# A segment sum in two levels: four 32-column matmuls and one that moves their result

## The chip, the cores and the metric

The kernel runs on one core of one Trainium2 chip. The metric is the device time of one execution in microseconds (us), of which the median over several runs is taken. Engines are named as in the profile: PE is TensorE's matmul, PEld its weight load, DVE is VectorE, ACT ScalarE, POOL GpSimd, SP SyncE.

## The reference

A graph layer (sum of the neighbours' features over 100,000 edges sorted by destination, 6,250 nodes of 256 features) and then a feed-forward layer with 8 experts, of which each node takes its best two.

```python
x = x + _L0_gnn_ref(_layernorm(x, axis=-1), W_self, W_neigh, b, src, dst)
x = x + _L0_ffn_ref(_layernorm(x, axis=-1)[None], gamma, beta, Wr, br, W1, b1, W2, b2)[0]

def _L0_gnn_ref(feat, W_self, W_neigh, b, src, dst):
    msg = feat[src]
    agg = jax.ops.segment_sum(msg, dst, num_segments=n)
    deg = jax.ops.segment_sum(jnp.ones_like(dst, dtype=feat.dtype), dst, num_segments=n)
    h_neigh = agg / jnp.maximum(deg, 1.0)[:, None]
    return feat @ W_self + h_neigh @ W_neigh + b

# feed-forward: the best 2 of 8 experts, weighted by a softmax over their two logits
logits = jnp.einsum('bsd,de->bse', xn, Wr) + br
h = jax.nn.gelu(jnp.einsum('bsd,dh->bsh', xn, W1[e]) + b1[e], approximate=False)
y_e = jnp.einsum('bsh,hd->bsd', h, W2[e]) + b2[e]
y = y + y_e * w_full[..., e, None]
```

All data are float32. The destinations are 6250 times the square of a uniform number, so edges lie dense at low nodes and thin at high ones.

## The kernel before

The edges stand in 784 columns of 128, sorted by destination. Four columns are a group (`GT = 4`), 196 groups in all, worked from the highest nodes down. POOL gathers a group's 512 source rows into a ring of four groups by four indirect DMAs (L689). DVE writes the group's one-hot matrices (L1257): for each edge a 1 in the column of its destination, counted from the group's first node (`target`), 128 columns wide. PE multiplies (L964): four accumulating matmuls give the sums of up to 128 nodes from the group's first on, and, from a column of ones, their degrees. DVE adds the result with two masks to the two blocks of 128 nodes that it may touch (`agg`, L1311), after which a block whose edges are all in is "finished": turned by PE (L952), multiplied with both weight matrices (L993, L995), normalised, routed (L1010), and its rows scattered to the experts' lists by POOL (L697).

Beside that run the experts. A unit is a tile of 128 listed rows with one expert, or a dense block with one expert. For each unit PE forms the hidden product (L1040, tiles and dense units alike), DVE adds the bias into `hid` (L1468), ACT applies gelu (L866), PE forms the result product (L1066 for tiles, L1074 for dense units), and DVE weighs it (L1477, L1479; L1499, L1503 for dense units). There is one hidden bank in PSUM, so a unit's hidden product waits for the bias of the unit before (`biased`). `hid` has two buffers.

What holds it together is a plan: `plan()` gives every step of every unit and block a slot, and each engine walks the slots in one loop, `for t in range(END)`, doing what falls into slot t in an order written out by hand. The 196 groups take slots 0 to 195. By these tables (`DENSE_STEPS`, `TILE_STEPS`) a unit's bias stands one slot after its hidden product; for the last 50 tiles both stand in the same slot. 143 of the 196 slots hold a hidden product, and 66 of these products stand in the slot in which DVE adds the bias of the unit before. A plan's slot has no fixed length; an engine passes on to the next as its waits allow.

The order inside a slot is: on PE turns, hidden product, places, router, block products, result product, and last the group sum; on DVE one-hots for group t+2, block steps, the bias, lists, choices, block sums, the weighing, and last the addition of group t-1 (`group_sums`). Groups 0 to 5 (`RAW`) are normalised by ACT after the gather. `claims()` at slot 3 counts edges that don't fit the assumptions about spans; were there any, a repair path would redo all edges.

## Time and profile before

| | us |
|---|---|
| median of 3 runs (1587.45, 1588.26, 1598.54) | 1588.26 |
| span of the profiled execution, first to last instruction | 1546.9 |
| PE busy | 1199.9 (78%) |
| DVE busy | 867.0 (56%) |
| ACT busy | 426.8 (28%) |
| POOL busy | 944.1 (61%) |
| mean granted TensorE clock | 0.908 |

The profiled execution's own time is not reported apart from these runs; its span is 41.4 us under their median. The busy time of an engine is a sum over its instructions in that one execution. A matmul's end is modelled and overlaps the next one's start. An fp32 matmul is listed as two records (x8 for four matmuls).

### The profile page before, as it was taken

The numbers are of one execution on the slowest core, as the hardware profiler recorded it, in microseconds if no ns is written. First come the engines' busy times: TensorE is split into PE (matmuls) and PEld (weight loads), VectorE is DVE, ScalarE is ACT, GpSimd is POOL, SyncE is SP. The second block draws the span as 40 slices with busy tenths as digits, with TensorE's granted clock in tenths as the row PEclk, the third lists the DMA queues.
The fourth block names the chain that finished last, engine by engine and source line by source line (L and its number), as shares of the span: only waits on it lengthen the run. The fifth ranks groups of instructions, "written<-read, shape, count | busy, mean of one in ns | idle before, by whom it ended". The sixth has DMA issues, their size and how long they took to land.

```text
span 1546.9 us, 22459 instructions
## 1 busy us (share of the span) xinstructions
PE 1199.9 (78%) x6492; PEld 1041.8 (67%) x6493; DVE 867.0 (56%) x2814; ACT 426.8 (28%) x803; POOL 944.1 (61%) x1023
## 2 busy tenths in 40 slices
PE   0377988888977798989889888677858775879857
PEld 0266777867866676877778777566747764778747
DVE  6745556665564655656565565554636553545426
ACT  5412222222322332332332323213313210211111
POOL 6756656666566666566655657665665566666642
PEclk9788999999997899999999999788978897999979
DMA  9798777755454565555554555464565556656545
GB/s 335 232 297 247 244 230 239 238 166 173 152 166 124 164 190 160 181 172 171 188 182 157 181 157 164 135 191 133 165 204 157 167 158 199 201 165 222 167 139 175
DMA packets 175355, 289.69 MB, mean 187 GB/s; under 512 B 25600, under 2 KB 105344, under 8 KB 175104
## 3 DMA queue, kind: packets, MB, share of 16 engines
q1 hardware_dynamic: 124288, 156.38, 30.6%
q0 software_dynamic: 45504, 124.36, 27.3%
q10 hardware_dynamic: 5440, 7.47, 1.4%
q8 instruction: 57, 0.93, 0.2%
q14 instruction: 66, 0.54, 0.1%
HBM read 231.43 MB, written 56.68 MB: 186 GB/s over the span
## 4 chain that ended last, share of the span: by engine, by line
PE 33%; DVE 28%; another core or an unknown queue 21%; issue 12%; DVEq 2%; POOL 2%; DMA 1%; SPq 0%; ACT 0%; POOLq 0%; ACTq 0%
PE bank L1040 9%; PE bank L964 8%; PE bank L1066 6%; DVE agg L1311 5%; PE bank L1074 4%; DVE heap L1468 4%; DVE onehot L1257 3%; PE bank L952 2%; PE bank L993 1%; PE bank L995 1%; DMA heap<-in_x 1%; DVE nstats L1339 1%; DVE xf L1334 1%; DVE agg L1337 1%
## 5 line engine op out<-in xcount | busy, mean ns | idle before, releaser
L689 POOL DMA_INDIRECT ring<-feature_table,src_sb x760 | 742.3, 977 | 468.3 <-issue 194.6
L964 PE MATMUL bank<-ring,onehot 128*128 128x257 f32 x1552 | 404.0, 403 | 73.5 <-DMA rows<-in_x,src_sb 40.9
L964 PEld LDWEIGHTS bank<-ring,onehot 128*128 128x128 f32 x1552 | 312.1, 203 | 131.7 <-issue 83.4
L1468 DVE TENSOR_TENSOR heap<-bank,b_sb 128x512 f32<-128x512 f32 x145 | 100.1, 690 | 342.1 <-remote 249.7
L1066 PE MATMUL bank<-heap 128*128 x712 | 193.5, 418 | 60.4 <-issue 18.1
L1040 PE MATMUL bank<-row_t,heap 128*128 128x128 f32 x1424 | 195.9, 294 | 38.8 <-DVE heap L1468 19.3
L1040 PEld LDWEIGHTS bank<-row_t,heap 128*128 128x128 f32 x1424 | 186.6, 208 | 46.2 <-issue 45.0
L866 ACT ACTIVATE heap<-heap 128x512 f32<-128x512 f32 x145 | 91.6, 632 | 453.7 <-DVE heap L1468 312.7
L1066 PEld LDWEIGHTS bank<-heap 128*128 128x128 f32 x712 | 142.4, 208 | 86.0 <-issue 66.3
L1040 PE MATMUL bank<-dst_i,heap 128*128 128x128 f32 x896 | 115.8, 284 | 32.8 <-DVE heap L1468 25.9
L1257 DVE TENSOR_TENSOR onehot<-iota,target 128x512 f32<-128x512 f32 x196 | 134.3, 685 | 6.9 <-DVE xf L1328 3.5
L1040 PEld LDWEIGHTS bank<-dst_i,heap 128*128 128x128 f32 x896 | 109.8, 198 | 41.4 <-issue 39.1
L1311 DVE SCALAR_TENSOR_TENSOR agg<-bank,in_first,agg 128x257 f32 x196 | 94.3, 481 | 75.1 <-remote 37.7
L1074 PE MATMUL bank<-heap 128*128 128x256 f32 x448 | 116.4, 404 | 21.3 <-DVE agg L1503 8.1
L859 ACT ACTIVATE row_t<-bank,gb_sb 128x128 f32<-128x128 f32 x178 | 71.8, 455 | 179.0 <-remote 106.6
L697 POOL DMA_INDIRECT expert_rows<-rows,slots_of x82 | 83.5, 1019 | 50.1 <-issue 23.0
L1074 PEld LDWEIGHTS bank<-heap 128*128 128x128 f32 x448 | 86.4, 201 | 35.8 <-issue 25.0
L1311 DVE SCALAR_TENSOR_TENSOR agg<-bank,in_second,agg 128x257 f32 x196 | 93.3, 476 | 0.0
L993 PE MATMUL bank<-wn_sb,sums_t 128*128 128x256 f32 x196 | 56.5, 411 | 18.8 <-issue 10.4
L844 ACT ACTIVATE normal_t<-bank,gb_sb 128x128 f32<-128x128 f32 x84 | 33.8, 452 | 130.7 <-remote 91.0
L826 ACT ACT_TABLE_LOAD x47 | 60.3, 1283 | 0.8
L866 ACT ACT_TABLE_LOAD x46 | 59.0, 1283 | 0.8
(190 smaller groups left out, 1258.1 us busy)
## 6 DMA issues: line engine op xcount, KB each, us to landing
heap<-in_w SPq DMA_DIRECT2D x145, 512.0 KB
expert_out<-empty_row SPq DMA_DIRECT2D x68, 256.0 KB
ring<-feature_table,src_sb POOLq DMA_INDIRECT x760
row<-expert_rows SPq DMA_DIRECT2D x89, 128.5 KB
xf<-in_x SPq DMA_DIRECT2D x49, 128.0 KB
ff<-feature_table SPq DMA_DIRECT2D x49, 128.0 KB
expert_out<-inside SPq DMA_DIRECT2D x45, 128.0 KB
expert_out<-y_out SPq DMA_DIRECT2D x44, 128.0 KB
```

The source lines that it names most:

```text
L689: pool.indirect_dma_start(group_row(t, i)[:, 0:D], None, x if t < RAW else table, bass.IndirectOffsetOnAxis(src_sb[:, k:k + 1], 0)).then_i ...
L697: pool.indirect_dma_start(rows_tab, bass.IndirectOffsetOnAxis(slots_at(S, n)[:, c:c + 1], 0), rows[s][:, c, :], None).then_inc(S.scattered ...
L859: last = act.activation(row_t[s][:, k, :], turned_b[:, k * P:(k + 1) * P], ACT.Identity, bias=gb_sb[:, 1, k:k + 1], scale=gb_sb[:, 0, k:k ...
L866: act.activation(hid[s], hid[s], ACT.Gelu).then_inc(S.gelu, 1)
L964: last = pe.matmul(bank[t % 2][:, 0:D + 1], onehot[:, q, i, :], group_row(t, i), start=(i == 0), stop=(i == GT - 1))
L993: pe.matmul(product_b[:, D:2 * D], t[:, k, :], wn_sb[:, k, :], start=(k == 0), stop=(k == DK - 1))
L1040: last = pe.matmul(hidden_b[:, c * P:(c + 1) * P], w1_of[w][:, k, c * P:(c + 1) * P], turned[:, k, :], start=(k == 0), stop=(k == DK - 1))
L1066: last = pe.matmul(result_b[:, 0:D], hid[s][:, k, :], w2_sb[:, k, bass.ds(e, 1), :].rearrange("p o d -> p (o d)"), start=(k == 0), stop=(k ...
L1074: last = pe.matmul(result_b[:, 0:D], hid[unit_of_dense[u] % 2][:, k, :], w2_sb[:, k, u % NE, :], start=(k == 0), stop=(k == HK - 1))
L1257: dve.tensor_tensor(onehot[:, q, :, :], iota[:, :].unsqueeze(1).broadcast_to([P, GT, P]), target[:, g * GT:(g + 1) * GT].unsqueeze(2).broa ...
L1311: last = dve.scalar_tensor_tensor(out=a, in0=bank[t % 2][:, 0:D + 1], scalar=mask[:, g:g + 1], in1=a, op0=ALU.mult, op1=ALU.add)
L1468: dve.tensor_tensor(hid[S.slot(u, 2)], hidden_b[:, :].rearrange("p (k t) -> p k t", k=HK), b1_sb[:, bass.ds(e, 1), :].rearrange("p o k -> ...
```

## The change

A group is now summed in two levels. For each of its four columns i PE multiplies with a one-hot of 32 columns only (`tile_hot`, counted from the column's own first node, `SPAN = 32`) and writes the result to the partitions 32 i to 32 i + 31 of bank 0. ACT copies these 128 rows to SBUF (`copy_partial`). A fifth matmul (`move`), with a one-hot of 128 columns (`node_hot`) that says for each of the 128 rows which node of the group it is, adds them up at their node rows in bank 1, and DVE adds bank 1 to `agg`. Bank 0 and bank 1 were the two buffers of the group sum before; each has one role now.

The order changes with it. On PE `group(t)` stands first in slot t and `move(t)` last. On ACT `copy_partial(t)` stands first in slot t. On DVE the addition of group t-1 stands first in slot t from slot 6 on (before, last). The one-hots of a later group wait for `moved` where they waited for `summed`. In the head the first nodes of all 784 columns are spread over the partitions, and `claims()` finds misfits by maxima and minima of two differences.

```diff
         onehot_flat = onehot[:, :, :, :].rearrange("p a b c -> p (a b c)")
+        tile_hot = [onehot_flat[:, q * P:(q + 1) * P].rearrange("p (i m) -> p i m", i=GT) for q in range(GS)]
+        node_hot = [onehot_flat[:, (GS + q) * P:(GS + q + 1) * P] for q in range(GS)]
+        partial = [onehot_flat[:, 2 * GS * P + s * (D + 1):2 * GS * P + (s + 1) * (D + 1)] for s in range(2)]
...
+            def copy_partial(t):
+                act.wait_ge(summed, t + 1)
+                if t >= 2:
+                    act.wait_ge(moved, t - 1)
+                act.copy(partial[t % 2], bank[0][:, 0:D + 1]).then_inc(copied, 1)
...
             for t in range(END):
+                if RAW - 2 <= t < NG:
+                    copy_partial(t)
                 for n in blocks_in(t, "copy"):
...
                 pe.wait_ge(gathered[q], 16 * GT * (t // GS + 1))
-                if t >= 2:
-                    pe.wait_ge(added, t - 1)
+                if t >= 1:
+                    pe.wait_ge(copied, t)
                 for i in range(GT):
-                    last = pe.matmul(bank[t % 2][:, 0:D + 1], onehot[:, q, i, :], group_row(t, i),
-                                     start=(i == 0), stop=(i == GT - 1))
+                    last = pe.matmul(bank[0][i * SPAN:(i + 1) * SPAN, 0:D + 1], tile_hot[q][:, i, :], group_row(t, i),
+                                     start=True, stop=True)
                 last.then_inc(summed, 1)
+
+            def move(t):
+                pe.wait_ge(copied, t + 1)
+                if t >= 1:
+                    pe.wait_ge(added, t)
+                pe.matmul(bank[1][:, 0:D + 1], node_hot[t % GS], partial[t % 2], start=True, stop=True).then_inc(moved, 1)
...
             for t in range(END):
+                if t < NG:
+                    group(t)
                 for n in blocks_in(t, "turn"):
...
                 if t < NG:
-                    group(t)
+                    move(t)
...
                 if t >= GS:
-                    dve.wait_ge(summed, t - GS + 1)
-                dve.tensor_tensor(onehot[:, q, :, :], iota[:, :].unsqueeze(1).broadcast_to([P, GT, P]),
-                                  target[:, g * GT:(g + 1) * GT].unsqueeze(2).broadcast_to([P, GT, P]),
-                                  ALU.is_equal).then_inc(hot_ready, 1)
+                    dve.wait_ge(moved, t - GS + 1)
+                dve.tensor_tensor(tile_hot[q], iota[:, 0:SPAN].unsqueeze(1).broadcast_to([P, GT, SPAN]),
+                                  target[:, g * GT:(g + 1) * GT].unsqueeze(2).broadcast_to([P, GT, SPAN]), ALU.is_equal)
+                dve.tensor_scalar(node_hot[q], iota[:, :], place[:, g:g + 1], None, ALU.is_equal).then_inc(hot_ready, 1)
...
             def claims():
-                link(dve.tensor_scalar(inside[:, :], inside[:, :], -1.0, 1.0, ALU.mult, ALU.add))
-                link(dve.tensor_reduce(n_missed[:, 0:1], inside[:, :], AX.X, ALU.add))
+                link(dve.tensor_tensor(inside[:, :].rearrange("p (g t) -> p g t", t=GT), dst_i[:, :].rearrange("p (g t) -> p g t", t=GT),
+                                       base_i[:, :].unsqueeze(2).broadcast_to([P, NG, GT]), ALU.subtract))
+                dve.tensor_reduce(reached[:, 0:1], target[:, :], AX.X, ALU.max)
+                dve.tensor_reduce(reached[:, 1:2], target[:, :], AX.X, ALU.min)
+                dve.tensor_reduce(reached[:, 2:3], inside[:, :], AX.X, ALU.max)
+                link(dve.tensor_reduce(reached[:, 3:4], inside[:, :], AX.X, ALU.min))
...
                 g = NG - 1 - t
-                dve.wait_ge(summed, t + 1)
+                dve.wait_ge(moved, t + 1)
...
-                    last = dve.scalar_tensor_tensor(out=a, in0=bank[t % 2][:, 0:D + 1], scalar=mask[:, g:g + 1],
+                    last = dve.scalar_tensor_tensor(out=a, in0=bank[1][:, 0:D + 1], scalar=mask[:, g:g + 1],
...
             for t in range(END):
-                if t == NG:
+                if t == NG or RAW <= t < NG:
                     group_sums(t)
...
-                if 1 <= t < NG:
+                if 1 <= t < RAW:
                     group_sums(t)
```

On PE, slot 80 before (L1040 is the hidden product, L1074 the result product of a dense unit, L964 the group sum; the first rows are the end of slot 79):

```order
L1066 MATMUL bank<-heap 128x256
L964 MATMUL bank<-ring,onehot 128x257 [waits added,gathered3,hot_ready]
L964 MATMUL bank<-ring,onehot 128x257 x3
L1040 MATMUL bank<-dst_i,heap 128x128 [waits p_biased,p_w1_in0]
L1040 MATMUL bank<-dst_i,heap 128x128 x7
L1074 MATMUL bank<-heap 128x256 [waits p_c_y,p_gelu]
L1074 MATMUL bank<-heap 128x256 x3
L964 MATMUL bank<-ring,onehot 128x257 [waits added,gathered0,hot_ready]
L964 MATMUL bank<-ring,onehot 128x257 x3
```

The same place after (L985 is the first level, L993 the move, L1067 the hidden product, L1093 and L1101 result products):

```order
L1093 MATMUL bank<-heap 128x256
L993 MATMUL bank<-onehot 128x257 [waits added,copied]
L985 MATMUL bank<-ring,onehot 32x257 [waits copied,gathered0,hot_ready]
L985 MATMUL bank<-ring,onehot 32x257 x3
L1067 MATMUL bank<-dst_i,heap 128x128 [waits p_biased,p_w1_in0]
L1067 MATMUL bank<-dst_i,heap 128x128 x7
L1101 MATMUL bank<-heap 128x256 [waits p_c_y,p_gelu]
L1101 MATMUL bank<-heap 128x256 x3
L993 MATMUL bank<-onehot 128x257 [waits added,copied]
```

The group's own work moved from the slot's end to its start, and the move, which waits for ACT's copy and for DVE's addition of the group before, took the place at the end.

On DVE, end of slot 80 and start of slot 81 before (L1477 and L1479 weigh a result, L1311 adds a group sum, L1257 is the one-hot, L1468 the bias):

```order
L1477 TENSOR_TENSOR y_out<-bank,b_sb 128x256
L1479 TENSOR_SCALAR y_out<-y_out,row 128x256 [waits p_c_y]
L1311 ISA [waits added,summed,p_sums_turned]
L1311 SCALAR_TENSOR_TENSOR agg<-bank,in_first,agg 128x257
L1311 ISA
L1311 SCALAR_TENSOR_TENSOR agg<-bank,in_second,agg 128x257
L1257 TENSOR_TENSOR onehot<-iota,target 128x512 [waits summed]
L1468 TENSOR_TENSOR heap<-bank,b_sb 128x512 [waits p_hidden,p_result]
```

The same place after:

```order
L1516 TENSOR_TENSOR y_out<-bank,b_sb 128x256
L1518 TENSOR_SCALAR y_out<-y_out,row 128x256 [waits p_c_y]
L1350 ISA [waits added,moved,p_sums_turned]
L1350 SCALAR_TENSOR_TENSOR agg<-bank,in_first,agg 128x257
L1350 ISA
L1350 SCALAR_TENSOR_TENSOR agg<-bank,in_second,agg 128x257
L1286 TENSOR_TENSOR onehot<-iota,target 128x128 [waits moved]
L1288 TENSOR_SCALAR onehot<-iota,onehot 128x128
L1507 TENSOR_TENSOR heap<-bank,b_sb 128x512 [waits p_hidden,p_result]
```

The rows look alike, but the addition is another one: before, it took group 79, the last of slot 80's work; after, it takes group 80, as the first of slot 81's, and waits for the move that PE does last in slot 80.

## Rows read from the trace of the kernel before

**Rows 1.** The page: busy time by engine; the chain by engine.

```profile
PE 1199.9 (78%) x6492; PEld 1041.8 (67%) x6493; DVE 867.0 (56%) x2814; ACT 426.8 (28%) x803; POOL 944.1 (61%) x1023
...
PE 33%; DVE 28%; another core or an unknown queue 21%; issue 12%; DVEq 2%; POOL 2%; DMA 1%; SPq 0%; ACT 0%; POOLq 0%; ACTq 0%
```

**Rows 2.** Stretch 100 to 1480 us: busy PE, PEld, DVE, ACT, POOL; clock, DMA share, GB/s.

```profile
100.00:1480.00 1380.00, 1125.85 (x6136) 979.75 (x6136) 766.10 (x2438) 372.44 (x694) 851.35 (x869) 0.91 0.58 182
```

**Rows 3.** The additions of the group sums (line L1311): ns, first and last start.

```profile
L1311 DVE SCALAR_TENSOR_TENSOR agg<-bank,in_first,agg x196: 465/482/488, 61.0 to 1477.9; 128x257 f32 x196
```

**Rows 4.** Timeline of PE, 583 to 594 us: start, us, engine, line, instruction.

```profile
583.78 1.90 PE L964 MATMUL bank<-ring,onehot 128*128 128x257 f32 x8
587.20 2.02 PE L1040 MATMUL bank<-dst_i,heap 128*128 128x128 f32 x16 [1.52 <-DVE heap L1468]
589.06 1.89 PE L1074 MATMUL bank<-heap 128*128 128x256 f32 x8
590.78 1.90 PE L964 MATMUL bank<-ring,onehot 128*128 128x257 f32 x8
592.53 1.72 PE L1040 MATMUL bank<-row_t,heap 128*128 128x128 f32 x14
```

**Rows 5.** Groups by line: count, busy us, mean ns, idle before and its causes.

```profile
L689 POOL DMA_INDIRECT ring<-feature_table,src_sb x760 | 742.3, 977 | 468.3 <-issue 194.6 <-PE bank L964 151.7 <-remote 117.5
...
L821 ACT COPY sums_t<-bank 128x512 f32<-128x512 f32 x49 | 28.2, 575 | 89.9 <-PE bank L952 54.9 <-remote 33.4 <-issue 1.7
```

**Rows 6.** Timeline of PE, 705.5 to 707.5 us, around the one-column weights of L1027.

```profile
706.16 0.38 PE L952 MATMUL bank<-ident,row 128*128 128x128 f32 x2
706.48 0.20 PE L1027 MATMUL bank<-placed_so_far,ones 128*1 128x8 f32 x2
706.60 0.44 PE L952 MATMUL bank<-ident,rows 128*128 128x128 f32 x2
706.88 0.82 PE L964 MATMUL bank<-ring,onehot 128*128 128x257 f32 x3
```

**Rows 7.** Timeline of DVE, 583 to 594 us.

```profile
583.39 0.69 DVE L1257 TENSOR_TENSOR onehot<-iota,target 128x512 f32<-128x512 f32 x1 [0.43 <-DVE xf L1328]
584.00 0.16 DVE L1348 RECIPROCAL nscale<-nscale 128x1 f32<-128x1 f32 x1
...
586.36 0.69 DVE L1468 TENSOR_TENSOR heap<-bank,b_sb 128x512 f32<-128x512 f32 x1 [1.75 <-remote]
...
589.06 0.48 DVE L1311 SCALAR_TENSOR_TENSOR agg<-bank,in_first,agg 128x257 f32 x1
...
589.85 0.68 DVE L1257 TENSOR_TENSOR onehot<-iota,target 128x512 f32<-128x512 f32 x1
590.99 0.69 DVE L1468 TENSOR_TENSOR heap<-bank,b_sb 128x512 f32<-128x512 f32 x1 [0.45 <-PE bank L1074]
...
592.89 0.49 DVE L1311 SCALAR_TENSOR_TENSOR agg<-bank,in_first,agg 128x257 f32 x1 [0.30 <-PE bank L964]
```

**Rows 8.** Timeline of PE before the first and the last of the 66 products.

```profile
132.73 0.38 PE L952 MATMUL bank<-ident,agg 128*128 128x128 f32 x2
...
134.31 2.02 PE L1040 MATMUL bank<-dst_i,heap 128*128 128x128 f32 x16 [0.98 <-DVE heap L1468]
...
983.38 0.38 PE L952 MATMUL bank<-ident,row 128*128 128x128 f32 x2
983.59 1.61 PE L1040 MATMUL bank<-row_t,heap 128*128 128x128 f32 x13
```

**Rows 9.** Timeline of DVE in the head.

```profile
55.77 1.41 DVE L1227 BATCH_NORM_STATS2 stats<-ring 128x6 f32<-128x256 f32 x4 [6.05 <-POOL agg L679]
...
69.06 0.97 DVE L1293 TENSOR_REDUCE n_missed<-inside 128x1 f32<-128x784 f32 x1
```

**Rows 10.** Who waited for whom: us in total, times, longest.

```profile
DVE heap L1468 <- remote: 249.7, 59, 17.1
...
PE bank L1040 <- DVE heap L1468: 45.2, 23, 7.6
```

More of the change, by code:

```diff
@@ L811, in _ @@
             raw_root_of(3)
-            raw_normal(2)
-            raw_normal(3)
-            for t in range(4, RAW):
-                raw_root_of(t)
-                raw_normal(t)
+            for t in range(RAW - 2):
+                copy_partial(t)
+                raw_normal(t + 2)
+                if t + 4 < RAW:
+                    raw_root_of(t + 4)
             def copy_sums(S, n):
@@ L946, in _ @@
             pe.wait_ge(base_ready, 1)
-            pe.matmul(product_b[:, 0:NG], ones[0:1, :], base_f, start=True, stop=True).then_inc(base_bc, 1)
+            pe.matmul(product_b[:, 0:NT // 2], ones[0:1, :], tile_base[:, 0:NT // 2], start=True, stop=True)
+            pe.matmul(sums_b[:, 0:NT // 2], ones[0:1, :], tile_base[:, NT // 2:NT], start=True, stop=True)
+            of_group = tile_base.rearrange("o (g i) -> o g i", i=GT)
+            for i in range(GT):
+                last = pe.matmul(hidden_b[i * SPAN:(i + 1) * SPAN, 0:NG], ones[0:1, 0:SPAN], of_group[:, :, i], start=True, stop=True)
+            last.then_inc(ramp_products, 1)
             pe.wait_ge(ring_ones, 1 + 2 * (RAW - GS))
@@ L1278, in _ @@
+            link(last)
             one_hots(0)
@@ L1527, in group_sums @@
                 hold(main.sums_turned, len([n for n in range(LAST) if block_at["turn"][n] <= t]))
-                beside = [u for u in range(EARLY) if DENSE_BLOCKS[u // NE] == LAST - 1 and dense_at["sum"][u] <= t]
+                beside = [u for u in range(EARLY) if DENSE_BLOCKS[u // NE] == LAST - 1 and dense_at["sum"][u] < t]
                 if beside:
@@ L1591, in _ @@
                     if DENSE_BLOCKS[u // NE] == LAST - 1:
-                        dve.wait_ge(added, t - 1)
+                        dve.wait_ge(added, min(t, NG))
                     early_sum(u)
```

59 lines of the change are left out of this document (36 added, 23 removed).

## Prediction

> **What bounds the kernel now.** I read the page first (busy shares, the 40 slices, the chain), then the groups by line, then the waits, then stretches of the timeline. The span is 1546.9 us, and PE is busy for 78% of it, DVE 56%, ACT 28%, POOL 61% [rows 1]. The median of the timed runs is 1588.26 us, so 41.4 us lie around the span; the sum below is made on the span and added to the median. The stage that matters runs from about 100 to 1480 us: PE is busy 1125.85 of 1380 us there, with a granted clock of 0.91 [rows 2]. The chain that ended last gives PE 33% and DVE 28% of the span [rows 1]. So no engine is full: PE leads, and DVE, which adds the biases and the group sums, stands between its pieces.
>
> The program goes by slots, one edge group in each. They take about 7.27 us each, from the first addition at 61.0 to the last at 1477.9 [rows 3]. A slot of the common kind reads so on PE [rows 4]: hidden product (587.20 to 589.06), result product (589.06 to 590.78), group sum (590.78 to 592.53). These are starts: each lasts until the next one starts, 1.86, 1.72 and 1.75 us, though the listed durations are some 0.17 us longer, because a matmul's tail overlaps the next. I take 1.74 us for the group sum: eight records, 0.217 us each.
>
> POOL was busy 742.3 us with 760 gathers and spent 194.6 us between them, 1.23 us for one and 4.9 us for a group [rows 5]; 82 scatters come beside. It waited 151.7 us for L964 and 117.5 us for something that the profile doesn't name. It is no bound at a slot of 7.27 us, but it is the floor of a light slot.
>
> **Part 1, PE time of a group.** The four 128-column matmuls go, with their 1.74 us. In come four with 32 columns of weights and one of 128 that moves the result. Each fp32 matmul is two records, and the stream is as long as before, 257 columns, so one record still takes 0.217 us. If nothing overlaps, the first level costs 8 x 0.217 = 1.74 us and the move 0.43 us: +0.43. If matmuls in different column quarters may run at once, but the two records of one matmul may not, then in issue order each second record runs beside the next matmul's first: five record times, 1.09 us, and with the move 1.52 us. If all eight pack by fours it is 0.43 + 0.43 = 0.87 us. No row shows two narrow matmuls side by side. I take the middle one, since records stand in order in every row of the trace and the two of one matmul share their quarter.
>
> Changing the width of the weights is not free. The only narrow weights are the one-column ones of L1027 [rows 6]: the two records of L952 before them should end 0.22 us after 706.16, they start at 706.48 (0.10 late), and behind them two records of L952 take 0.28 in place of 0.22 (0.06 late). In and out together that is 0.16 us; the bound from below is zero, from above twice that, as the new weights are 32 columns wide and loaded eight times. So 1.52 + 0.16 = 1.68 against 1.74: **-0.06 us** for a slot in which PE sets the pace. Some 120 such slots: **-7 us**.
>
> The Trainium skill speaks of this twice. TensorE: Matmul & The Clock Gate, section "Measured speedup vs the span model", has three column tiles together 2.38 times as fast as one by one, and a span of one matmul and about 4 ns for each further tile; taken at its word, that is the full packing above. TensorEngine Tiling (Array Packing), section "Key Properties", says that changing the tiling mode drains the engine, which is a price on every slot, twice. No run here shows either yet; the 0.16 us of L1027 is the nearest.
>
> **Part 2, the new order on DVE.** This is the term I trust most. Until now DVE adds group t-1 at the end of its slot t. Now, from group 6 on, it does so at the slot's start, ahead of the one-hots and of the bias, and it waits there for the move, PE's last work in slot t-1. PE's next hidden product waits for that bias, since there is one hidden bank. The old order shows at 590.99 [rows 7]: the bias starts before PE has finished the group sum (to 592.53 [rows 4]), and the hidden product follows without a gap. In the new order the bias can't start until all this is over, from the moment the move has left the array: 0.17 us to its listed end and 0.2 us to DVE (an addition starts at 592.89, and the group before it was listed to 590.78 + 1.90 = 592.68 [rows 4, 7]); two additions 0.79 us (589.06 to 589.85); the one-hots 0.55 us (an instruction over 512 elements lists 0.69 us and one over 257 lists 0.48, 0.8 ns an element, so 128 take 0.3 less than 0.61, the step from start to start of 512, and there are two now); 0.69 us for the bias, 0.15 us to PE (586.36 + 0.69 to 587.20); one slot in four has a load of window numbers too. Together 2.55 us; I take 2.5.
>
> By the plan's tables 66 hidden products stand in the slot whose DVE part holds the bias of the one before (slots 16 to 134; the last 50 tiles run bias and product in one slot and are spared). Read from the end of the group in the array to the start of the hidden product, these 66 had a mean of 1.02 us. The first of them reads 1.58 (132.73 to 134.31) and the last 0.21 (983.38 to 983.59) [rows 8]; two between read 1.68 (585.52 to 587.20) and 0.0 (592.53) [rows 4]. Taking 2.5 wherever it was shorter gives a mean of 2.60. A slot held before 1.02 + 1.74 us outside the hidden and result products; now it holds 2.60 + 0.43 (move) + 0.16. The narrow matmuls themselves disappear in the 2.60. That is 3.19 against 2.76: +0.43 us, times 66, **+29 us**. Between 2.3 and 2.9 for the chain this is +16 and +52 us. The cover for the first level is gone only if it costs over some 2 us.
>
> **Part 3, ACT.** It copies 128 x 257 once a group. A copy of 128 x 512 from PSUM takes 0.575 us [rows 5]; for half the width I take 0.42 us (0.29 to 0.57), 82 us in all on an engine with 28%. It stands first in ACT's slot. Behind it wait the copies of turned rows and the gelu; but the bias that the gelu needs comes 2.5 us after the slot's start, the copy is done by about 1.9 us (1.09 sum, 0.2, 0.42, 0.2). The move waits for it at the slot's end, 3.5 us later. In slots without hidden product it can show, yet those go by POOL's 4.9 us. Cost 0; upper bound 0.4 us in 43 slots, +17 us.
>
> **Part 4, DVE's work.** One-hots shrink by some 0.1 us a slot, 20 us of DVE's 867; on the path of Part 2 they are counted. Gain elsewhere 0 to 10 us; I take 0.
>
> **Part 5, the head.** Before the first one-hots DVE has six passes over 784 columns, which become shorter. It gains nothing, since DVE then idles 6.05 us for POOL [rows 9]. But the claims at group 3 grow: out go two passes over 784 columns, 1.6 us together, in come five at 1.0 us (the reduction there takes 0.97 us and a gap [rows 9]) and four small ones at 0.2. PE's group 4 waits behind it. +4.2 us, bounds 0 and 5: **+4 us**.
>
> Sum: -7 + 29 + 4 = +26 us, 1588.26 + 26 = **1614 us**.
>
> **Rivals.** *No overlap of the quarters* (slower). The group then costs 1.74 + 0.43 + 0.16 = 2.33 us, +0.6 in each slot that PE paces, 77 (the others with a hidden product) to 120 of them: +46 to +72, with the 29 and the 4: 1667 to 1693. *The wait on the move is taken up* by stalls that are there anyway: PE idles some 250 us between 100 and 1480, and 249.7 us of waits before DVE's bias have no named cause [rows 10]. If the added wait falls into these, about 1585 to 1592. *The change falls into the repair path*, which redoes all edges, if a column of 128 edges spans 32 nodes; the widest spans 26 with these inputs, so under 1%.
>
> **Chances.** Forecast's mechanism with 1600 to 1650: 0.42. No overlap or a dearer switch, 1650 to 1700: 0.18. Full packing or another gain, under 1572: 0.2. Taken up, within 1% (about what this measurement can tell, 16 us): 0.18, and a part of the first case's low edge. That gives faster 0.21, same 0.19, slower 0.60. The range leaves out some 0.1 at each end: 1552 to 1690.
>
> **What the profile will show.** In the trace after: the first level from its start to the next operation at 1.1 us (1.7: no overlap; 0.5: full). The bias of L1507 starting 1.6 to 1.9 us after the move ends in slots 16 to 134, and PE idle before L1067, released by DVE, at well over the 45.2 us of now [rows 10]. ACT near 500 us busy. If PE's idle time doesn't grow there, Part 2 is wrong. If the narrow records start 0.3 us or more after what precedes them, the switch was too cheap.

## Result: 17% slower, and the profile after

The changed kernel takes 1864.83 us (median of 4, 1860.88 to 1870.97), the kernel before 1589.47 us (1587.45 to 1598.54) beside it: ratio 1.1724, 95% interval 1.1685 to 1.1762. The prediction was 1614 us with a range to 1690: it had the sign and a tenth of the size.

One reading of the prediction falls at once. It took 41.4 us to lie "around the span". In the profiled execution after, 1866.13 us go with a span of 1864.4, so only 1.7 us do. The profiled execution of before was a quick one; a second gave 1558.62 us with a span of 1556.9 (e11 below). I compare the spans of profiles with each other, and times by their ratios. The two disagree by some 42 us, because of that quick execution: the spans grow by 317.5 us, the medians by 275.

The page after, busy time and chain, against [rows 1]:

```profile
PE 1210.0 (65%) x6894; PEld 920.2 (49%) x6895; DVE 821.6 (44%) x3020; ACT 489.1 (26%) x999; POOL 922.5 (49%) x1023
...
PE 25%; another core or an unknown queue 14%; DVE 12%; issue 8%; DVEq 2%; ACT 1%; DMA 0%; SPq 0%; ACTq 0%
```

The span grew by 317.5 us (1864.4 - 1546.9). PE's busy time grew by only 10.1 us, so 307.4 us are new idle time on PE, and DVE is less busy than before. ScalarE has 62 us more work (489.1 against 426.8) and is busy for 26%. No engine is near full; all engines wait more. The stretch from 100 us to 1800 us, columns as in [rows 2]:

```profile
100.00:1800.00 1700.00, 1144.33 (x6568) 875.93 (x6567) 727.57 (x2639) 434.11 (x886) 837.64 (x876) 0.82 0.49 150
```

PE is busy for 67% of it, where it was 82%, and the granted clock is 0.82 in place of 0.91. The groups by line:

```profile
L1067 PE MATMUL bank<-row_t,heap 128*128 128x128 f32 x1424 | 224.1, 320 | 94.3 <-DVE heap L1507 62.0 <-issue 31.8
...
L985 PE MATMUL bank<-ring,onehot 128*32 128x257 f32 x1552 | 149.9, 434 | 48.5 <-ACT ring L801 36.6 <-issue 11.9
L993 PE MATMUL bank<-onehot 128*128 128x257 f32 x392 | 143.0, 451 | 104.4 <-ACT onehot L820 49.8 <-issue 35.0 <-DVE agg L1350 19.6
...
L1350 DVE SCALAR_TENSOR_TENSOR agg<-bank,in_first,agg 128x257 f32 x196 | 94.9, 484 | 694.3 <-PE bank L973 270.3 <-PE bank L993 210.7 <-remote 143.1
...
L820 ACT COPY onehot<-bank 128x257 f32<-128x257 f32 x196 | 72.9, 372 | 980.5 <-PE bank L985 517.9 <-remote 403.1 <-issue 31.5
```

First level (L985) and move (L993) list 292.9 us together. The four wide matmuls of before listed 404.0 us:

```profile
L964 PE MATMUL bank<-ring,onehot 128*128 128x257 f32 x1552 | 404.0, 403 | 73.5 <-DMA rows<-in_x,src_sb 40.9 <-issue 22.3 <-ACT ring L793 10.2
```

So the edit to the matmuls did save PE time. All other PE work, nearly the same instructions as before, lists 1040.9 us in place of 923.5, added up over all lines: 117 us more, at the lower clock. (Such a sum counts twice where a tail overlaps the next line's start, before and after alike.) DVE stands idle before the addition (L1350) for 694.3 us, until PE's turns (L973) or the move (L993) in the waits that the row names most. ScalarE stands 980.5 us before the copy (L820), but is busy for only 26% of the span.

One slot on PE, and on DVE beside it (start, us, engine, line, instruction, idle before):

```profile
704.90 0.60 PE L993 MATMUL bank<-onehot 128*128 128x257 f32 x2
705.43 0.64 PE L985 MATMUL bank<-ring,onehot 128*32 128x257 f32 x8
706.00 0.44 PE L973 MATMUL bank<-ident,agg 128*128 128x128 f32 x2
706.28 0.38 PE L973 MATMUL bank<-ident,ff 128*128 128x128 f32 x2
706.50 0.38 PE L973 MATMUL bank<-ident,row 128*128 128x128 f32 x2
708.82 2.02 PE L1067 MATMUL bank<-row_t,heap 128*128 128x128 f32 x16 [1.95 <-DVE heap L1507]
...
712.91 1.99 PE L1093 MATMUL bank<-heap 128*128 x8 [1.72 <-DVE agg L1542]
714.74 0.60 PE L993 MATMUL bank<-onehot 128*128 128x257 f32 x2
```

```profile
706.80 0.48 DVE L1350 SCALAR_TENSOR_TENSOR agg<-bank,in_first,agg 128x257 f32 x1 [9.40 <-PE bank L973]
...
707.99 0.68 DVE L1507 TENSOR_TENSOR heap<-bank,b_sb 128x512 f32<-128x512 f32 x1
...
711.51 0.48 DVE L1542 SCALAR_TENSOR_TENSOR agg<-bank,spread,agg 128x256 f32<-128x256 f32 x1
...
715.65 0.49 DVE L1350 SCALAR_TENSOR_TENSOR agg<-bank,in_first,agg 128x257 f32 x1 [2.94 <-issue]
```

Read the two together and they are one line, not two. DVE stands until PE has done the move, the next first level and the turns (706.80); then PE stands until DVE has added, made the one-hots and done the bias (708.82); PE waits again before the results (712.91, the row names DVE); DVE waits for the move (715.65: the row names no cause, but the move is listed from 714.74 to 715.34). The slot takes 9.84 us, from move to move (704.90 to 714.74). In [rows 4, 7] the bias at 590.99 runs under PE's group sum, and the addition comes behind it.

The first level takes 0.57 us from its start to the next (705.43 to 706.00) for eight records, and the move 0.53 (704.90 to 705.43) for two. So the eight records take little more than two would one by one. The group costs PE 1.10 us, where it cost 1.74 [rows 4].

From such timelines I worked out every slot's length, from the end of one group (or move) to the next, for slots 10 to 195:

```
                                   before     after     added in all
66 slots, bias before the product  7.31 us    9.57 us   149 us
77 others with a hidden product    8.21       9.37       90
43 without a hidden product        6.26       7.68       61
head, to the end of group 9        93.5      110.4       17
```

That is 316 of the 317.5 us, after rounding. The prediction had +29 us in the first row, -7 us in the next two together, and +4 us in the head.

### The profile page after: what moved, and what is told of

Read it like the earlier page. It is cut to its first block, busy times and chain, and to the rows that moved or that the text cites. A ratio compares the mean times of both kernels' runs of the same rounds, so it can differ in the third digit from the quotient of the medians.

```text
span 1864.4 us, 24065 instructions
## 1 busy us (share of the span) xinstructions
PE 1210.0 (65%) x6894; PEld 920.2 (49%) x6895; DVE 821.6 (44%) x3020; ACT 489.1 (26%) x999; POOL 922.5 (49%) x1023
## 4 chain that ended last, share of the span: by engine, by line
PE 25%; another core or an unknown queue 14%; DVE 12%; issue 8%; DVEq 2%; ACT 1%; DMA 0%; SPq 0%; ACTq 0%
PE bank L1067 7%; PE bank L1093 5%; PE bank L993 2%; DVE heap L1507 2%; DVE agg L1350 2%; PE bank L985 2%; PE bank L973 2%; PE bank L1101 2%; PE bank L1020 1%; PE bank L1022 1%; DVE onehot L1286 1%; DVE onehot L1288 1%; ACT normal_t L858 1%; DVEq L184 1%
## 5 line engine op out<-in xcount | busy, mean ns | idle before, releaser
L1350 DVE SCALAR_TENSOR_TENSOR agg<-bank,in_first,agg 128x257 f32 x196 | 94.9, 484 | 694.3 <-PE bank L973 270.3
L820 ACT COPY onehot<-bank 128x257 f32<-128x257 f32 x196 | 72.9, 372 | 980.5 <-PE bank L985 517.9
L1067 PE MATMUL bank<-row_t,heap 128*128 128x128 f32 x1424 | 224.1, 320 | 94.3 <-DVE heap L1507 62.0
L1067 PEld LDWEIGHTS bank<-row_t,heap 128*128 128x128 f32 x1424 | 209.3, 232 | 111.4 <-issue 99.3
L1093 PE MATMUL bank<-heap 128*128 x712 | 207.6, 439 | 61.8 <-issue 28.3
L993 PE MATMUL bank<-onehot 128*128 128x257 f32 x392 | 143.0, 451 | 104.4 <-ACT onehot L820 49.8
L1093 PEld LDWEIGHTS bank<-heap 128*128 128x128 f32 x712 | 151.4, 222 | 93.7 <-issue 71.0
L1067 PE MATMUL bank<-dst_i,heap 128*128 128x128 f32 x896 | 141.4, 323 | 79.2 <-DVE heap L1507 55.7
L985 PE MATMUL bank<-ring,onehot 128*32 128x257 f32 x1552 | 149.9, 434 | 48.5 <-ACT ring L801 36.6
L1067 PEld LDWEIGHTS bank<-dst_i,heap 128*128 128x128 f32 x896 | 132.0, 234 | 96.6 <-issue 96.6
L1101 PE MATMUL bank<-heap 128*128 128x256 f32 x448 | 128.7, 437 | 34.3 <-DVE agg L1542 20.0
L993 PEld LDWEIGHTS bank<-onehot 128*128 128x128 f32 x392 | 80.8, 221 | 134.5 <-ACT onehot L820 66.7
L1101 PEld LDWEIGHTS bank<-heap 128*128 128x128 f32 x448 | 95.2, 222 | 51.1 <-issue 37.3
L985 PEld LDWEIGHTS bank<-ring,onehot 128*32 128x32 f32 x1552 | 35.1, 114 | 133.1 <-issue 131.9
L1350 DVE SCALAR_TENSOR_TENSOR agg<-bank,in_second,agg 128x257 f32 x196 | 93.2, 475 | 0.0
L1020 PEld LDWEIGHTS bank<-wn_sb,sums_t 128*128 128x128 f32 x196 | 42.4, 240 | 59.2 <-issue 54.5
```

Source lines behind the costliest of these rows:

```text
L820: act.copy(partial[t % 2], bank[0][:, 0:D + 1]).then_inc(copied, 1)
L985: last = pe.matmul(bank[0][i * SPAN:(i + 1) * SPAN, 0:D + 1], tile_hot[q][:, i, :], group_row(t, i), start=True, stop=True)
L993: pe.matmul(bank[1][:, 0:D + 1], node_hot[t % GS], partial[t % 2], start=True, stop=True).then_inc(moved, 1)
L1020: pe.matmul(product_b[:, D:2 * D], t[:, k, :], wn_sb[:, k, :], start=(k == 0), stop=(k == DK - 1))
L1067: last = pe.matmul(hidden_b[:, c * P:(c + 1) * P], w1_of[w][:, k, c * P:(c + 1) * P], turned[:, k, :], start=(k == 0), stop=(k == DK - 1))
L1093: last = pe.matmul(result_b[:, 0:D], hid[s][:, k, :], w2_sb[:, k, bass.ds(e, 1), :].rearrange("p o d -> p (o d)"), start=(k == 0), stop=(k ...
```

## Experiments

Three theories went in. **A**: the new order makes PE's slot and DVE's slot take turns. **B**: the data path of the two levels (one bank for each level, ScalarE's copy, the fifth matmul). **C**: the prediction's own step, the wait for the bias alone.

### Which part of the change

**e2**: the kernel before, with the addition moved to the start of DVE's slot and nothing else; the lines left out fit two counts of other waits to the new place.

```diff
-                if t == NG:
+                if t == NG or RAW <= t < NG:
                     group_sums(t)
...
-                if 1 <= t < NG:
+                if 1 <= t < RAW:
                     group_sums(t)
...
```

> The kernel before with one thing of the change alone: DVE adds group t-1 at the start of its slot t (from slot 6 on), ahead of the one-hots and the bias; sums in one level as before. Theory A (the order on DVE makes PE's slot and DVE's slot follow each other in turn, so every DVE result that PE needs comes late, not the bias alone): most of the +275 us, 1780 to 1900. Theory B (the data path costs it: one bank for each level, ACT's copy, the fifth matmul): within 2% of 1589. Theory C (my prediction's step, only the bias behind the addition): 1610 to 1640.

Measured: 1847.35 us, ratio 1.155 (1.1461 to 1.1639). **e1** is the complement, the changed kernel with the addition back at the slot's end (the same lines, the other way).

> The changed kernel with the addition back at the end of DVE's slot, as before; PE's order is the changed one, so the move at the end of PE's slot t waits for the addition at the end of DVE's slot t. Theory A: better than 1865, since bias, weighing and choices are free again, but the one bank behind the move ties PE's slot end to DVE's slot end: 1650 to 1780. Theory B: stays at 1830 to 1880. Theory C: 1590 to 1620.

Measured: 1740.14 us, ratio 1.0927 (1.0849 to 1.1005). So the addition's place costs 15.5 points by itself, without a narrow matmul in sight, but 9.3 points remain when it is put back. The waits of e2, against [rows 10]:

```profile
DVE agg L1311 <- PE bank L964: 378.7, 85, 14.2
DVE agg L1311 <- PE bank L952: 217.8, 36, 10.2
PE bank L1040 <- DVE heap L1468: 201.3, 75, 8.4
```

Each engine waits for the other: DVE for the group sums and the turns, PE for the bias (45.2 us before).

**e6**: the changed kernel with the addition directly behind the bias; **e19**, later, the same edit to the kernel before. Both add a wait of DVE on its own earlier work.

```diff
...
                     hidden_bias(main, main.unit(j), of_tile[j])
+                if RAW <= t < NG:
+                    group_sums(t)
...
```

> The changed kernel with the addition moved behind the bias of the same slot on DVE; all else as changed. It frees the hidden product alone. Theory C: the whole excess goes, 1590 to 1620. Theory A: a part, since weighing, choices and block sums still stand behind the addition: 1760 to 1840. Theory B: 1850 to 1880.

> The kernel before, with the addition moved from the end of VectorE's slot to right behind the bias (at its start the ratio was 1.155). The bias no longer stands behind the addition; what stands behind it are choose, the sums of x1 and the weighing of results. Theory C (the bias alone pays for the new place): ratio 1.00 to 1.02. Theory A (whatever VectorE has behind a wait for TensorE's end of the slot before makes the two alternate): 1.03 to 1.07.

Measured: e6 1769.37 us, ratio 1.1091 (1.1022 to 1.1159); e19 1642.92 us, ratio 1.0541 (1.0473 to 1.0609). Taking the bias out from behind the addition brings 10 of the 15.5 points. The other 5.4 stay: work of DVE other than the bias pays too. The bias has most of it, not all. One place where it may show in e19 is ScalarE, which waits for DVE's statistics; the row of before comes first, that of e19 second:

```profile
ACT nscale L826 <- DVE nmv L1340: 88.0, 24, 15.8
ACT nscale L826 <- DVE nmv L1340: 171.8, 33, 16.5
```

**e15** and **e16** split e2 by slots: the addition at the slot's start only in the 66 slots that the prediction counted, or only in the others.

```diff
...
+            behind_bias = {b[0] for a, b in zip(runs_at, runs_at[1:]) if a[1] == b[0]}
+            at_start = {t for t in range(RAW, NG) if t in behind_bias}
...
-                if t == NG:
+                if t == NG or t in at_start:
                     group_sums(t)
...
```

> The kernel before, with the addition at the start of VectorE's slot only in those slots in which VectorE holds the bias that a hidden product of the same slot on TensorE waits for (the 66 of the prediction); in all others it stays at the slot's end. With it at the start of every slot the ratio to before was 1.155, some 245 us. Theory C (the prediction's step: all of the cost sits in these slots, only its size was too small): ratio 1.14 to 1.16. Theory A (TensorE and VectorE come to alternate in every slot): about the share of these slots in the loss of that run, two thirds: 1.09 to 1.12.

> The complement: the kernel before, with the addition at the start of VectorE's slot in all slots from group 6 on but those of the 66. Theory C: no loss, ratio 0.99 to 1.01. Theory A: the rest of the loss, 1.04 to 1.07.

Measured: e15 1743.73 us, ratio 1.1166 (1.1111 to 1.1221); e16 1641.12 us, ratio 1.0495 (1.0437 to 1.0552). They add up to 16.6 points against e2's 15.5. The slots that the prediction counted carry 70%; the others, which it had at zero, carry 30%.

### Banks and TensorE's order

**e7**: the kernel before, only the wait of a group on the additions is one group tighter, as `move(t)` has it in the changed kernel with its one bank.

```diff
-                if t >= 2:
-                    pe.wait_ge(added, t - 1)
+                if t >= 1:
+                    pe.wait_ge(added, t)
```

> The kernel before, with one edit: the group of slot t on TensorE waits until all groups before it are added, where it waited for all but the last. The two PSUM banks still alternate, the order of all engines is that of before; only the slack that two banks give is taken away, as the changed kernel's single second-level bank does. Theory S (the slack in slots between TensorE and VectorE is what the time hangs on, an order of the two engines being one way to lose it): TensorE at the end of its slot t now waits for the end of VectorE's slot t, where it waited for the end of slot t-1; the run with two levels and the addition back at the slot's end has that same wait and took 1740 us, so this one should land at 1690 to 1760 us. Theory B (what is left of the loss with the addition at the slot's end is the data path: the copy by ScalarE and the fifth matmul): 1590 to 1620 us, the wait being nearly always met.

Measured: 1718.45 us, ratio 1.0821 (1.0737 to 1.0904). No instruction moved, and it costs 8.2 points. In the changed kernel the same count costs less, because there the addition that it waits for stands at the start of DVE's slot: the move idles 19.6 us for it (L993 above). The group's line in e7:

```profile
L964 PE MATMUL bank<-ring,onehot 128*128 128x257 f32 x1552 | 455.9, 444 | 304.9 <-DVE agg L1311 208.4 <-issue 55.5 <-DMA rows<-in_x,src_sb 41.0
```

Before, it idled 73.5 us there. PE at the end of slot t now waits for the end of DVE's slot t, where it waited for the end of slot t-1.

**e10**: the kernel before, with `group(t)` at the start of PE's slot (the last four stay).

```diff
             for t in range(END):
+                if t < NG - 4:
+                    group(t)
                 for n in blocks_in(t, "turn"):
...
```

> The kernel before, with only TensorE's order of the change: the group's four matmuls stand at the start of TensorE's slot instead of at its end (the last four groups excepted, which stay at the end); the addition stays at the end of VectorE's slot. Theory S: the group at the start of slot t waits for the addition at the end of VectorE's slot t-1, half a slot to a slot less slack than at its end, while VectorE gets the sums early: a small loss, 1595 to 1640 us. A rival (the loss came from VectorE's order alone; TensorE's order is neutral or a gain since the addition never waits for it): 1560 to 1592 us.

Measured: 1745.94 us, ratio 1.0976 (1.0909 to 1.1044), outside both expectations. The group's wait for the addition now stands at the head of PE's slot, and the turns, the hidden product and the results queue behind it:

```profile
L964 PE MATMUL bank<-ring,onehot 128*128 128x257 f32 x1552 | 449.7, 439 | 293.9 <-DVE agg L1313 182.2 <-issue 61.5 <-DMA rows<-in_x,src_sb 40.5
```

**e8** gives e1 both banks for both levels: first level and move of a group share bank t mod 2, and the first level waits for the addition of the group before last.

```diff
-                if t >= 1:
-                    pe.wait_ge(copied, t)
+                if t >= 2:
+                    pe.wait_ge(added, t - 1)
...
-                if t >= 1:
-                    pe.wait_ge(added, t)
-                pe.matmul(bank[1][:, 0:D + 1], node_hot[t % GS], ...
+                pe.matmul(bank[t % 2][:, 0:D + 1], node_hot[t % GS], ...
...
```

> The kernel with two levels and the addition back at the end of VectorE's slot (1740 us), with one more edit: the first level of group t and its move both use bank t mod 2, so that TensorE waits for the addition of the group before last, as before the change, and the move waits only for the copy. Theory S: the slack is back, so the time falls to 1590 to 1640 us; what is left is the copy's way through ScalarE. Theory B: the single bank was not the cost, 1720 to 1745 us.

Measured: 1695.93 us, ratio 1.0685 (1.0597 to 1.0773), against 1.0927 of e1. Part came back, 2.4 points or 44 us, and not the 100 us or more that were expected: the wait is gone from the move, but in this order it stands before the first level, at the head of the slot, as in e10:

```profile
L985 PE MATMUL bank<-ring,onehot 128*32 128x257 f32 x1552 | 157.3, 449 | 216.4 <-DVE agg L1348 105.3 <-issue 58.3 <-DMA rows<-in_x,src_sb 36.7
```

**e3** instead keeps the order of before and moves the second level a slot later: group at the end of PE's slot t, copy at the start of ScalarE's slot t+1, move behind hidden in PE's slot t+1, addition at the end of DVE's slot. **e9** is e3 with the banks of e8.

```diff
...
                     hidden_of_rows(main, j)
+                if 1 <= t <= NG:
+                    move(t - 1)
...
                 if t < NG:
-                    move(t)
+                    group(t)
...
-                if RAW - 2 <= t < NG:
-                    copy_partial(t)
+                if RAW - 2 <= t - 1 < NG:
+                    copy_partial(t - 1)
...
```

> Two levels with slack: the first level at the end of PE's slot t, ACT's copy at the start of its slot t+1, the move behind the hidden product in PE's slot t+1, the addition at the end of DVE's slot t+1 as in the kernel before. PE's own cost of a group is about 1.1 us (0.57 and 0.53 between starts in the changed kernel) against 1.74. Theory A: at least as good as before, 1530 to 1590. Theory B: 1700 or more. Theory C: 1550 to 1600.

> The kernel with the group at the end of TensorE's slot t, ScalarE's copy at the start of its slot t+1, the move behind hidden in TensorE's slot t+1 and the addition at the end of VectorE's slot (1636 us), with one more edit: first level and move of a group use bank t mod 2, so that the first level waits for the addition of the group before last and the move for the copy alone. Theory S: all slack of the kernel before is back and TensorE has 0.64 us less work in each of 196 slots: 1540 to 1590 us. Theory B (the ScalarE copy in the chain and a lower TensorE clock cost what is left): 1610 to 1640 us, as without the edit.

Measured: e3 1636.44 us, ratio 1.0251 (1.0187 to 1.0314); e9 1626.26 us, ratio 1.0261 (1.0188 to 1.0333). With the slack given back 15 of the 17 points are gone. The second bank brought nothing more here, and a kernel with less PE work (1154.7 us busy in e9, 1199.9 before) is still slower than before.

### What is left: the hop and the worth of PE's time

**e14**: the kernel before with only the hop: ScalarE copies the bank onto itself at the start of its next slot, and the addition waits for that too.

```diff
+                if RAW - 2 <= t - 1 < NG:
+                    act.wait_ge(summed, t)
+                    act.copy(bank[(t - 1) % 2][:, 0:D + 1], bank[(t - 1) % 2][:, 0:D + 1]).then_inc(copied, 1)
...
+                if t >= RAW - 2:
+                    dve.wait_ge(copied, t + 1 - (RAW - 2))
```

> The kernel before, with the group still in four 128-column matmuls at the end of TensorE's slot, plus a hop through ScalarE as the two levels have it: at the start of its slot t+1 ScalarE waits for group t, copies the bank onto itself (257 columns), and VectorE's addition at the end of its slot waits for this copy too. No sixth matmul and no move. Theory H (the hop through ScalarE costs what is left when slots and banks are as before): 1610 to 1640 us. Theory V (what is left comes from the move's place on TensorE, not from ScalarE): 1585 to 1600 us.

Measured: 1601.42 us, ratio 1.0252 (1.0153 to 1.035): as much as e3 and e9 have left. ScalarE is busy for only 481.0 us in e14. What the hop costs seems to be less its time than its place: in its fixed order ScalarE now stands waiting for PE's group, with its other work behind. No run separates the two cleanly. Its waits in e14:

```profile
ACT bank L889 <- PE bank L967: 396.4, 90, 11.3
ACT bank L889 <- remote: 372.8, 60, 13.5
```

Two more place the parts of e9 anew: **e12** moves the move further down, ahead of the results; **e17** moves the copy up, ahead of ScalarE's roots and shares.

> The kernel with both banks alternating and the move behind hidden (1626 us), with the move put further down TensorE's slot, ahead of the results, so that ScalarE has longer for the copy. In that run TensorE idled 140 us ahead of the move, mostly for the copy, and VectorE 350 us ahead of the addition. Theory H (ScalarE's copy comes late for the move): 1590 to 1615 us. Theory V (VectorE's addition comes late as the move is late; moving it down moves the wait over to VectorE): 1625 to 1660 us.

> The kernel with both banks alternating and the move behind hidden (ratio 1.0261), with ScalarE's copy of group t moved up from the start of its slot t+1 to behind the gelu of slot t, ahead of the shares, roots and second rows, which wait for VectorE. Theory H (the hop's cost is ScalarE's lag behind VectorE when TensorE asks for the move): ratio 1.00 to 1.015. Theory J (the hop costs whatever ScalarE's order is, since TensorE and VectorE each wait one more step): 1.02 to 1.03.

Measured: e12 1627.21 us, ratio 1.0387 (1.0297 to 1.0478), no gain; e17 1666.91 us, ratio 1.066 (1.0608 to 1.0712), 4 points worse than e9 and outside both expectations. So the place of the copy matters. Now the roots stand behind it, and DVE waits for them (2.0 us in e9):

```profile
DVE nscale L1385 <- ACT nscale L840: 106.4, 30, 8.1
```

**e18** asks what PE's time was worth: two more 128-column matmuls ahead of each group of the kernel before, overwritten by it. **e13** and **e20** issue the packed first level twice in e9, and three times in the changed kernel.

```diff
+                for i in range(2):
+                    pe.matmul(bank[t % 2][:, 0:D + 1], onehot[:, q, i, :], group_row(t, i), start=True, stop=True)
                 for i in range(GT):
...
```

> The kernel before, with two more 128-column matmuls ahead of each group of four (their result is overwritten): 0.87 us more TensorE work in each of 196 slots, 170 us. Theory W (TensorE's work is what a slot of before lasts by, so that 0.64 us less of it would have brought 50 to 90 us): ratio 1.06 to 1.10. Theory K (the slot of before hangs on other things, and the work that the two levels save was worth little): ratio 1.00 to 1.03.

> The kernel with both banks alternating and the move behind hidden (1626 us), with the four packed matmuls of the first level issued twice over, the second set writing the same values again. It adds 0.45 to 0.6 us of TensorE work to each of 196 slots, 90 to 115 us. Theory W (TensorE's work of a slot is on the path): 1700 to 1740 us. Theory K (the path is the waits between the engines, and TensorE's granted clock, 0.867 here and 0.908 before, is low because TensorE has gaps; more work fills them and the clock rises): 1600 to 1650 us, clock 0.89 or more.

> The changed kernel, with the four packed matmuls of the first level issued three times over, which adds 0.9 to 1.2 us of TensorE work to each slot, 180 to 240 us. In the changed kernel (ratio 1.1724) TensorE idles some 600 us, and the work that both kernels share takes 121 us longer at a granted clock of 0.831 than at 0.908. Theory K (the low clock is what TensorE gets for its gaps; more work in the gaps brings the clock back, and most of the added work is hidden under the wait for the bias): ratio 1.15 to 1.19, clock 0.87 or more. Theory W: the added work counts, 1.24 to 1.30, clock as before.

Measured: e18 1598.24 us, ratio 1.0221 (1.0171 to 1.0272), clock 0.930; e13 1613.23 us, ratio 1.0294 (1.0212 to 1.0376), clock 0.893; e20 1884.13 us, ratio 1.2076 (1.2011 to 1.2141), clock 0.864. The page of e18 and its two group lines:

```profile
PE 1337.7 (84%) x7276; PEld 1170.9 (73%) x7277; DVE 867.8 (54%) x2814; ACT 426.3 (27%) x803; POOL 936.0 (59%) x1023
```

```profile
L966 PE MATMUL bank<-ring,onehot 128*128 128x257 f32 x1552 | 390.6, 392 | 18.9 <-issue 18.7
L964 PE MATMUL bank<-ring,onehot 128*128 128x257 f32 x776 | 217.4, 403 | 59.8 <-DMA rows<-in_x,src_sb 41.0 <-issue 9.9 <-ACT ring L793 8.6
```

A group takes 2.61 us from start to start where it took 1.74, 170 us more in 196 slots, and the kernel is 35 us slower (2.2% of 1566.43): some 0.2 us for each. (The two rows list 608.0 us together, but tails overlap in that sum.) Most of the added work went into PE's gaps: against the first profile of before PE is busy 138 us more (1337.7 against 1199.9) and idle 86 us less (261.2 against 347.0). A smaller part is the clock: PE's other work, added up over its lines, lists 895.3 us in place of 923.5, at a granted clock of 0.930 in place of 0.908. So PE's work is cheap in the kernel before, though PE is busy for 78% of it. By that price the 125 us that two levels save (0.64 in each of 196 slots) were worth some 26 us, an estimate from this one direction.

In e13 86 us more of L985 (233.6 against e9's 147.6) moved the ratio by 0.3 points, within the intervals. e20 fell between its two expectations. Its three sets list 194 us more than one, PE's other work falls from 1040.9 to 997.3 us with the clock at 0.864, and still the kernel is 3.5 points slower: with the gaps filled the clock came back in part, but it didn't pay.

**e11**: the kernel before again, for a second profile.

> The kernel before, unchanged, for a second profiled execution of it. The first has a span of 1546.9 us and a mean granted clock of 0.908, some 40 us under the median of its timed executions, while the changed kernel's span and median agree. If that was chance, this one has a span of 1575 to 1600 us at a clock of 0.88 to 0.90; if a profiled execution of this kernel is always quicker, about 1547 us again.

Measured: 1558.62 us, span 1556.9, clock 0.905, between the two expectations. Executions of before lay between 1552.92 and 1606.69 us in the five comparisons, with medians from 1562.47 to 1597.07, so the first profile, with the shortest span of all, was a quick execution. What makes one quick isn't shown. Its busy times repeat within 2 us (PE 1198.2, DVE 866.6).

## Why the prediction was wrong

**Part 2, the addition's place, was the step that failed**, mechanism right, size wrong by far. It forecast a chain of 2.5 us from the end of the move to the hidden product in 66 slots, a mean of 2.60. Measured in these slots: some 3.8 us after, 3.1 in e2, against 1.0 before. Two links were left out. The addition also waits for PE's turns of the same slot (the semaphore `sums_turned`), which stood out of its way at the slot's end: it starts at 706.80 in place of 705.7 above. (In 36 waits, 270.3 us, the turns came last, but that is not their price: of the 9.40 us above 8.3 would have been idle without them.) And `normal` stands between the one-hots and the bias in some slots. The one-hots erred the other way: their own numbers give 0.6 us where the sum has 0.55, and they took 0.4 (from 706.80 + 0.79 to 707.99). The longer chain makes some 80 of the 120 us that these 66 slots lost beyond the forecast; the rest lies in waits further down the slot, as at 712.91. What the prediction meant as the check of the sum, PE before L1067 released by DVE "well over the 45.2 us", reads 117.7 us:

```profile
PE bank L1067 <- DVE heap L1507: 117.7, 52, 6.7
```

**The larger error was to price one wait and not the loop.** A slot is a loop: DVE waits for PE's slot before, PE for DVE's. By the counts of its waits the old order left about one slot of slack on either side. The prediction looked at who waits behind the bias, and gave everything else on DVE no price. e16 (5.0 points in slots held at zero) and e19 (5.4 points with the bias ahead) show that it had one. Even the slots of the last 50 tiles, which the prediction called spared, grew from 8.10 to 9.67 us; 48 of them lie among the 196, which makes 75 us.

**Two edits of the diff were never priced.** `move(t)` waits for `added, t` where `group(t)` waited for `added, t - 1`, and the group went to the head of PE's slot. Alone on the kernel before they cost 8.2 (e7) and 9.8 points (e10), each five to six times the whole forecast of 1.6. The single costs, 15.5 + 9.8 + 8.2 + 2.5, add up to 36 points and the change has 17.2. That fits one slack which all of them use up, but these prices hold for an addition at the slot's end. With the addition first (e2, 15.5 points) all the rest of the change together adds 1.7 points; no run took it apart in that order.

**Part 1** took the middle case (five record times). The rival of full packing was right: 0.57 us for eight records, and in e20 24 records take 1.44 us from start to start, so each further set of eight takes 0.435 us, the time of two. That agrees with the span of one matmul in the Trainium skill (TensorE: Matmul & The Clock Gate, "Measured speedup vs the span model"), which the prediction quoted and didn't follow. The changed kernel's timeline from 705.2 to 705.5 us alone shows how: four records start together, and the other four start only behind that window.

```profile
705.43 0.42 PE L985 MATMUL bank<-ring,onehot 128*32 128x257 f32 x4
```

In e20:

```profile
704.67 1.51 PE L985 MATMUL bank<-ring,onehot 128*32 128x257 f32 x24
706.11 0.44 PE L973 MATMUL bank<-ident,agg 128*128 128x128 f32 x2
```

The prediction had let each matmul's two records stand in line, one pair behind the other. The change of width was put at 0.16 us in and out; the move's 0.53 us less two records of 0.217, and the first set's 0.57 less 0.435, give 0.10 and 0.135. The rival's 1536 to 1566 us was wrong for another reason: it valued a PE microsecond at one, and e18 puts it near 0.2.

**Part 3** put ScalarE's copy at 0 with an upper bound of 17 us. The copy itself was cheaper than taken (0.372 us), but the hop costs 2.5 points in e14, some 39 us, and e17 shows that it hangs on the order. **Part 4** took no gain from DVE's shorter work. DVE is busy 45 us less and the kernel is slower; no run tests the saving by itself. **Part 5** had +4 us for the head, for the claims, and these grew by 4.6 us (7.3 to 11.9). But 7 us are lost by the end of group 5 and 17 by the end of group 9. What the rest comes from wasn't tested; copy and move stand in these groups too.

Open is how much of the loss the clock causes by itself: the other PE work lists 117 us more in the changed kernel, but no run changed the clock without changing gaps or work. Not tried is more slack than before by a third bank; all eight are in use. No version run here beat the kernel before.

## What to carry to other kernels

When engines work through one fixed order slot by slot, write down for each wait in which slot it is produced and in which, and where in the slot, it is consumed; follow the loop around through all engines, and price a change by the slack it takes from the loop, not by the one consumer that is named. A tighter semaphore count or a bank given up can cost as much as any instruction.

A busy share of 78% doesn't say that the engine's work is on the path. Adding work to it is a cheap test before work is taken away: here 170 us more cost 35.

## What the runs showed of the hardware

Four fp32 matmuls with 32-column weights into four quarters of the PSUM partitions ran in the time of one, both records of each included (0.435 us for eight records of 257 columns, where a wide record takes 0.217). Switching between 128- and 32-column weights cost 0.10 and 0.135 us by the differences above, not the 0.3 us or more that the prediction kept as a warning.

The granted clock was higher where PE's work was packed more closely: 0.930 with more work (e18), 0.908 before, 0.831 in the changed kernel. More work alone raised it from 0.867 (e9) to 0.893 (e13), and from 0.831 to 0.864 (e20). Behind 2.51 us of idle time a hidden product took 3.43 us, where it took 2.02 at 708.82. The granted clock was 0.59 in the stretch of the long one, so mostly the lower of the two levels (1.2 and 2.4 GHz), and 1.00 around the short one (columns as in [rows 2]):

```profile
718.42 3.43 PE L1067 MATMUL bank<-dst_i,heap 128*128 128x128 f32 x16 [2.51 <-issue]
...
718.40:722.00 3.60, 3.58 (x18) 3.58 (x19) 1.75 (x9) 1.31 (x3) 2.69 (x4) 0.59 0.47 130
705.00:714.00 9.00, 5.33 (x42) 4.19 (x41) 5.59 (x20) 2.58 (x4) 2.97 (x3) 1.00 0.30 86
```
